# Sequence half of a two-block kernel: two chunks mixed in one operation, and a new order on every engine

## The chip, the cores and the metric

The program runs on one core of a Trainium2 chip. The metric is the device time of the whole program in microseconds (us), as a median of several executions. The matrix engine (TensorE, PE in the rows), the vector engine (VectorE, DVE), the scalar engine (ScalarE, ACT), GpSimd (POOL) and SyncE (SP, which here issues DMAs) each run their own list of instructions in order, and wait for each other by semaphores.

## The reference, cut to what matters

The first half (a spectral gate and a 3x3 convolution) is not touched. Its result z, 512 image rows of 128 positions with 128 channels, goes into the second half:

```python
u = _layernorm(z, ln1_w, ln1_b).reshape(-1, na, e)
y = _mamba2(u, ...)            # below
z = z + _wn_linear(y, ff_g, ff_v, ff_b)
h = gelu(_wn_linear(_layernorm(z, ln2_w, ln2_b), fc1...))
return z + _wn_linear(h, fc2...)

def _mamba2(u):
    z_gate, xBC, dt = split(u @ in_proj_w.T)
    x, Bm, Cm = split(silu(conv1d(xBC, 4 taps) + conv_b))
    dt = softplus(dt + dt_bias);  A = -exp(A_log)
    # scan over positions: h = h*exp(dt*A) + dt*x*B;  y = h.C
    y = _ssm_scan(x, dt, A, Bm, Cm) + D_param * x
    yg = y * silu(z_gate)
    yn = yg * rsqrt(mean(yg**2) + LN_EPS) * ssm_norm_w
    return yn @ out_proj_w.T
```

One row of 128 positions is one sequence ("chunk") with 8 heads of 32 channels and 64 states. The scan is computed as matrices: for each head a 128x128 matrix of decays exp(difference of running sums) times the cross products C.B, and then this matrix times dt*x.

## The kernel before, in words

The sequence half works on groups of four chunks, 128 groups in all. One step of its loop takes one new group in, and holds four groups at different ages: `p` (newest), `a_`, `b`, `c` (oldest). Each engine has a function `body` that lists its operations of one step in a hand-written order; `pipeline` writes out eight steps ahead of the loop, runs the loop with two steps in its body, and writes out the last ones. So the order of `body` is the order on the engine, and every operation begins with waits on semaphores that others raise. `held(...)` is such a wait for a buffer to be free again.

On the path of a group (a number in brackets is the chunk of the four, 0 to 3, or a pair of chunks, 0 or 1):

- DVE `stats_in`, `moments_in`; POOL `root`, `norm_u`: first layer norm. PE `turn_u`, ACT `affine_u`: transposed to `ut`.
- PE `project_x(0)`, `project_x(1)`, `project_bc`, `project_z(0)`, `project_z(1)` (one 128x512 product each) and `project_dt`.
- ACT `tap`, `second_tap`, DVE `taps(j, 2)`, `taps(j, 3)`, POOL `add_tap(j)`: the four taps of the convolution for j = 0, 1 (x) and 2 (B and C); ACT `silu_*`.
- DVE and ACT: the small steps of softplus; PE `cumulate` (running sums), DVE `high`, `low`, `right`, POOL `left`: operands of the decays.
- PE `decays(g)`, ACT `exps(g)`, PE `cross`, DVE `weigh(g)`: the weighted 128x1024 matrix `mmat` of chunk g. PE `turn_x(pair)`, DVE `scale_x(pair)`: `dtx`.
- PE `mix(g)`: eight products of `mmat` and `dtx`, one per head, 32 output partitions each, so four of them stand beside each other in the array. A fp32 product is two instructions in the trace, so a `mix` has 16.
- DVE `gate(pair)`; ACT `squares`, POOL `add_squares`, PE `sums`, DVE `variance`, POOL `root_y`; PE `project_out`; DVE `residual`.
- DVE `stats_mid`, `moments_mid`, POOL `root`, `norm_h`, PE `turn_h`, ACT `affine_h`, PE `ffn1`, ACT `gelu`, PE `ffn2`, DVE `finish`, SP `store`.

The eight PSUM banks are shared by hand: a table of numbers says which product is written to which bank, and several `held` waits exist only because two products share one. In the rows a line number names the operation; on PE L1084 is `mix`, L1013 `project_x`, L1018 `project_bc`, L1027 `project_z`, L1006 `turn_u`, L1109 `turn_h`, L1114 `ffn1`, L1120 `ffn2`, L1053 `turn_x`, L1069 and L1072 `decays`, L1044 `cross`. On DVE L1424 is `residual`, L1315 the statistics, L1329 and L1437 `moments_in` and `moments_mid`, L1345 `add_bias`, L1339 `taps`, L1396 `weigh`, L1406 and L1412 `gate`, L1373 `high`, L1377 `low`, L1382 `right`, L1417 `variance`. On POOL L914 is `add_tap`, L909 `add_squares`, L921 `left`, L955 `add_ffb`, L927 `root_y`, L932 and L934 `root`, L946 and L950 `norm_h`.

## Time and profile before

| | us |
|---|---|
| median of 3 runs | 4249.27 (4245.84 to 4251.49) |
| profiled execution | 4248.45 |
| its span, first to last instruction | 4246.5 |
| granted TensorE clock, mean | 0.976 |

```profile
PE 3975.6 (94%) x31687; PEld 2858.3 (67%) x31687; DVE 3487.8 (82%) x8772; ACT 3152.6 (74%) x4936; POOL 2582.5 (61%) x2713
PE   7998899899989994899999999999999999999998
DVE  4568557754876384899999999999999999999997
ACT  4445534553555253899999999999999999999997
POOL 0036104600560065688888888888888888888886
```

The first row gives busy time, share of the span and instructions of each engine (PEld is the load of a matrix into TensorE, which lies beside PE's products). The others cut the span into 40 equal slices of 106 us; a digit is the busy share in tenths. The sequence half begins in the 17th slice, at about 1700 us, and is even to the end.

### The profile page before, as it was taken

How to read it: one execution, taken by the hardware profiler on the slowest of the kernel's cores; microseconds unless marked ns; L12 is line 12 of the kernel's file. 1: busy time of each engine (PE TensorE's matmuls, PEld its weight loads, DVE VectorE, ACT ScalarE, POOL GpSimd, SP SyncE). 2: the span in 40 equal slices, each digit the busy share in tenths (PEclk: the TensorE clock that was granted, in tenths of full speed). 3: DMA queues.
4: the chain of work that ended last, by engine and by line, in shares of the span. 5: the costliest groups of instructions: out<-in, count | busy, mean ns of one | idle time of the engine just before them, and what ended most of it. 6: DMA issues, size and time to landing. Idle time of an engine off the chain costs nothing.

```text
span 4246.5 us, 94479 instructions
## 1 busy us (share of the span) xinstructions
PE 3975.6 (94%) x31687; PEld 2858.3 (67%) x31687; DVE 3487.8 (82%) x8772; ACT 3152.6 (74%) x4936; POOL 2582.5 (61%) x2713
## 2 busy tenths in 40 slices
PE   7998899899989994899999999999999999999998
PEld 4787578758875883566666666666666666666665
DVE  4568557754876384899999999999999999999997
ACT  4445534553555253899999999999999999999997
POOL 0036104600560065688888888888888888888886
PEclk9999999999999997999999999999999999999999
DMA  2013101400240022111111111111111111111110
GB/s 91 1 53 129 58 9 61 161 11 12 73 157 0 14 85 77 36 40 40 42 40 42 40 37 42 40 42 40 40 39 40 42 40 42 40 37 42 40 42 26
DMA packets 214857, 205.85 MB, mean 48 GB/s; under 512 B 14368, under 2 KB 149152, under 8 KB 214688
## 3 DMA queue, kind: packets, MB, share of 16 engines
q1 hardware_dynamic: 214688, 203.60, 14.8%
q8 instruction: 105, 1.72, 0.2%
q14 instruction: 64, 0.52, 0.0%
HBM read 136.45 MB, written 67.11 MB: 48 GB/s over the span
## 4 chain that ended last, share of the span: by engine, by line
PE 59%; ACT 0%; DVE 0%; POOL 0%; issue 0%; POOLq 0%; DVEq 0%; ACTq 0%
PE g_ps L1084 7%; PE g_ps L1069 6%; PE g_ps L1027 6%; PE g_ps L1013 5%; PE g_ps L1072 5%; PE g_ps L1101 5%; PE g_ps L1044 3%; PE g_ps L1114 3%; PE g_ps L1120 3%; PE g_ps L1093 3%; PE g_ps L1053 3%; PE g_ps L1018 3%; PE g_ps L1033 2%; PE g_ps L1109 2%; PE g_ps L1006 2%; PE g_ps L1038 1%
## 5 line engine op out<-in xcount | busy, mean ns | idle before, releaser
L1396 DVE TENSOR_TENSOR g_mmat<-g_emat,g_ps 128x1024 f32<-128x1024 f32 x512 | 598.9, 1210 | 1.3 <-PE g_ps L1044 1.3
L1235 ACT ACTIVATE g_emat<-g_ps 128x1024 f32<-128x1024 f32 x512 | 521.3, 1025 | 86.3 <-PE g_ps L1072 84.8
L1339 DVE SCALAR_TENSOR_TENSOR g_acc<-g_ps,g_conv_w,g_acc 128x504 f32<-128x504 f32 (+1 forms) x768 | 554.5, 722 | 10.9 <-ACT g_acc L1198 9.2
L914 POOL TENSOR_TENSOR g_acc<-g_acc,g_tap 128x508 f32<-128x508 f32 x384 | 482.2, 1270 | 126.1 <-DVE g_acc L1339 126.1
L654 POOL MEMSET f_s_hi<- 128x192 f32 x4 | 1.0, 258 | 761.0 <-PE f_ps L345 761.0
L1084 PEld LDWEIGHTS g_ps<-g_mmat,g_dtx 128*32 128x32 f32 x8192 | 192.8, 109 | 310.4 <-issue 213.4
L1069 PE MATMUL g_ps<-g_rz,g_l 128*128 128x512 f32 x1024 | 391.3, 463 | 1.6 <-DVE g_z L1424 1.6
L229 PE MATMUL f_ps<-f_s_hi,f_wf_hi 128*128 128x256 f32 x1152 | 360.6, 313 | 4.9 <-DVE f_s_lo L489 4.9
L1084 PE MATMUL g_ps<-g_mmat,g_dtx 128*32 128x128 f32 x8192 | 329.3, 279 | 0.0
L230 PE MATMUL f_ps<-f_s_lo,f_wf_hi 128*128 128x256 f32 x1152 | 326.6, 284 | 0.0
L424 ACT ACTIVATE f_s_hi<-f_ps 128x384 fp32r<-128x384 f32 x256 | 125.6, 491 | 270.5 <-PE f_ps L217 265.2
L231 PE MATMUL f_ps<-f_s_hi,f_wf_lo 128*128 128x256 f32 x1152 | 326.1, 283 | 0.0
L1072 PE MATMUL g_ps<-g_mask_b,g_ident_b 128*128 128x512 bf16 x1024 | 310.7, 385 | 0.0
L672 POOL TENSOR_TENSOR f_zout<-f_zout,f_gamma 128x512 f32<-128x512 f32 x128 | 163.8, 1279 | 240.6 <-ACT f_zout L444 240.1
L1198 ACT ACTIVATE g_acc<-g_ps,g_conv_b,g_conv_w 128x512 f32<-128x512 f32 x384 | 298.4, 777 | 14.5 <-PE g_ps L1018 1.5
L1101 PEld LDWEIGHTS g_ps<-g_wc,g_ygt 128*128 128x128 f32 x2048 | 248.6, 192 | 62.3 <-issue 62.3
L909 POOL TENSOR_TENSOR g_sqs<-g_sq 128x256 f32<-128x256 f32 x256 | 182.0, 731 | 167.8 <-ACT g_sq L1240 167.8
L217 PE MATMUL f_ps<-f_idft_h,f_inv 128*128 128x192 f32 x1024 | 220.6, 341 | 63.7 <-DVE f_s_lo L489 56.6
L934 POOL TENSOR_TENSOR g_r<-g_r,g_mhalf 128x4 f32<-128x4 f32 x256 | 265.4, 1037 | 21.3
L1027 PE MATMUL g_ps<-g_ut,g_wz 128*128 128x512 f32 x512 | 276.2, 621 | 1.7 <-DVE g_acc L1339 1.7
L1013 PE MATMUL g_ps<-g_ut,g_wx 128*128 128x512 f32 x512 | 274.3, 618 | 1.6 <-ACT g_ut L1190 1.6
L1203 ACT ACTIVATE g_tap<-g_ps,g_conv_w 128x512 f32<-128x512 f32 x384 | 262.0, 682 | 2.3 <-PE g_ps L1013 2.2
(193 smaller groups left out, 12319.1 us busy)
## 6 DMA issues: line engine op xcount, KB each, us to landing
f_xt<-in_x_cols SPq DMA_DIRECT2D x32, 1024.0 KB, 10.9
f_xres<-in_x SPq DMA_DIRECT2D x128, 256.0 KB, 2.8
z<-f_zout SPq DMA_DIRECT2D x128, 256.0 KB, 2.0
g_zin<-z SPq DMA_DIRECT2D x128, 256.0 KB, 2.6
g_zres<-z SPq DMA_DIRECT2D x128, 256.0 KB, 2.9
out<-g_outb SPq DMA_DIRECT2D x128, 256.0 KB, 2.9
f_wf_raw<-in_w_f SPq DMA_DIRECT2D x1, 576.0 KB, 7.1
g_wx<-in_in_proj_t SPq DMA_DIRECT2D x1, 192.0 KB, 2.4
```

The source lines that it names most:

```text
L229: pe.matmul(out, wf_hi[:, p, x, :], hi, start=(x == 0), stop=False)
L230: pe.matmul(out, wf_hi[:, p, x, :], lo, start=False, stop=False)
L914: pool.tensor_tensor(acc[:, j, :, 1:], acc[:, j, :, 1:], tap1[:, j, :, 0:P - 1], ALU.add).then_inc(add_p[j], 1)
L1013: pe.matmul(ps[:, X_BANK[j], :], wx[:, j * P:(j + 1) * P], ut[:, :], start=True, stop=True).then_inc(px_mm[j], 1)
L1027: pe.matmul(ps[:, Z_BANK[j], :], wz[:, j * P:(j + 1) * P], ut[:, :], start=True, stop=True).then_inc(pz_mm[j], 1)
L1069: pe.matmul(four(ps[:, D_BANK[g] + half, :]), l4[:, g, :], rz[:, 4 * half:4 * half + 4, :], start=True, stop=False)
L1072: mm = pe.matmul(four(ps[:, D_BANK[g] + half, :]), ident_b[:, :], mask_b[:, :].unsqueeze(1).to_broadcast([P, 4, P]), start=False, stop=True)
L1084: mm = pe.matmul(ps[low:low + HEADDIM, bank, at + j * P:at + (j + 1) * P], dtx[:, g // 2, at + HEADDIM * h:at + HEADDIM * (h + 1)], mmat[: ...
L1101: mm = pe.matmul(ps[:, OUT, g * P:(g + 1) * P], ygt[:, x.s, g, j, :], wc[:, j, :], start=(j == 0), stop=(j == 1))
L1235: act.activation(emat[:, g, :].rearrange("p (b n) -> p b n", b=2), ps[:, D_BANK[g]:D_BANK[g] + 2, :], ACT.Exp).then_inc(e_a[g], 1)
L1339: dve.scalar_tensor_tensor(out=acc[:, j, :, k:], in0=four(ps[:, bank, :])[:, :, 0:P - k], scalar=conv_w[:, j, 3 - k:4 - k], in1=acc[:, j, ...
L1396: dve.tensor_tensor(mmat[:, g, :].rearrange("p (h n) -> p h n", h=HEADS), emat[:, g, :].rearrange("p (h n) -> p h n", h=HEADS), ps[:, CB, ...
```

## The change

`mix` takes a pair of chunks instead of one: it waits for the weighted matrices of both, and issues its 16 products (32 instructions) without a wait in between. There are two of them in a step instead of four, and two semaphores instead of four. All assignments of products to banks but two (`BC_BANK` and `CB`) are changed, with the waits that they need, and every engine's `body` is written in a new order. No arithmetic is added or removed. The diff, cut to its core:

```diff
-        UT, HT, F1 = 5, 5, 0
-        X_BANK, BC_BANK, Z_BANK = (2, 1), 3, (1, 2)
-        CB, XT_BANK, D_BANK, Y_BANK = 6, (4, 2), (0, 0, 4, 4), (3, 4)
-        SS, OUT, F2 = 6, 5, 3
+        UT, HT, F1 = 4, 1, 1
+        X_BANK, BC_BANK, Z_BANK = (1, 0), 3, (5, 2)
+        CB, XT_BANK, D_BANK, Y_BANK = 6, (0, 4), (4, 4, 2, 2), (6, 5)
+        SS, OUT, F2 = 3, 6, 0
...
             def left(x):
                 pool.wait_ge(q_d, x.n + 1)
-                held(pool.wait_ge, sqs_p[1], x.n, QUADS)
-                held(pool.wait_ge, sqs_p[0], x.n, QUADS)
-                pool.wait_ge(add_p[1], x.n + 1)
+                pool.wait_ge(add_p[2], x.n + 1)
...
             def add_ffb(x):
                 pool.wait_ge(zres_in[x.s], x.half * 16 + 16)
+                held(pool.wait_ge, z2_d, x.n, QUADS)
...
             def project_z(x, j):
                 pe.wait_ge(ut_a, x.n + 1)
                 if j == 0:
-                    held(pe.wait_ge, e_a[1], x.n, QUADS)
-                    pe.wait_ge(conv_d[1], x.n * 2 + 2)
-                if j == 1:
-                    pe.wait_ge(conv_d[0], x.n * 2 + 2)
+                    held(pe.wait_ge, gate_d[1], x.n, QUADS)
...
-            def mix(x, g):
-                pe.wait_ge(m_d[g], x.n + 1)
-                pe.wait_ge(dtx_d[g // 2], x.n + 1)
-                if g == 2:
-                    pe.wait_ge(e_a[3], x.n + 1)
+            def mix(x, pair):
+                pe.wait_ge(m_d[2 * pair], x.n + 1)
+                pe.wait_ge(m_d[2 * pair + 1], x.n + 1)
+                pe.wait_ge(dtx_d[pair], x.n + 1)
+                if pair == 1:
+                    pe.wait_ge(e_a[1], x.n + 1)
+                for g in (2 * pair, 2 * pair + 1):
...
-                mm.then_inc(y_mm[g], 1)
+                mm.then_inc(y_mm[pair], 1)
...
             def gate(x, pair):
-                dve.wait_ge(y_mm[2 * pair + 1], x.n + 1)
+                dve.wait_ge(y_mm[pair], x.n + 1)
```

The decays, `turn_x`, `left` and the exponentials now belong to `a_` instead of `b`, that is, they stand at the end of a step instead of the head of the next.

On PE, the stretch of a step that has the mixing, before:

```order
L1013 MATMUL g_ps<-g_ut,g_wx 128x512
L1084 MATMUL g_ps<-g_mmat,g_dtx 32x128 x8
L1109 MATMUL g_ps<-g_ident,g_hn 128x128 x4
L1027 MATMUL g_ps<-g_ut,g_wz 128x512
L1084 MATMUL g_ps<-g_mmat,g_dtx 32x128 x8
L1114 MATMUL g_ps<-g_ht,g_wt 128x512
L1084 MATMUL g_ps<-g_mmat,g_dtx 32x128 x8
L1006 MATMUL g_ps<-g_ident,g_u 128x128 x4
L1084 MATMUL g_ps<-g_mmat,g_dtx 32x128 x8
L1027 MATMUL g_ps<-g_ut,g_wz 128x512
L1120 MATMUL g_ps<-g_wt,g_gl 128x128 x4
```

and now (L1087 is `mix`, L1016 `project_x(1)`, L1021 `project_bc`, L1113 `turn_h`, L1118 `ffn1`, L1123 `ffn2`, L1009 `turn_u`):

```order
L1016 MATMUL g_ps<-g_ut,g_wx 128x512
L1021 MATMUL g_ps<-g_ut,g_wx 128x512
L1027 MATMUL g_ps<-g_ut,g_wz 128x512
L1113 MATMUL g_ps<-g_ident,g_hn 128x128 x4
L1087 MATMUL g_ps<-g_mmat,g_dtx 32x128 x16
L1118 MATMUL g_ps<-g_ht,g_wt 128x512
L1087 MATMUL g_ps<-g_mmat,g_dtx 32x128 x16
L1027 MATMUL g_ps<-g_ut,g_wz 128x512
L1038 MATMUL g_ps<-g_tri,g_dta 128x128
L1123 MATMUL g_ps<-g_wt,g_gl 128x128 x4
L1009 MATMUL g_ps<-g_ident,g_u 128x128 x4
```

Four blocks of mixing have become two, with `ffn1` between them; three 128x512 products now stand side by side, and `turn_u` stands behind `ffn2`.

On DVE, from `low` to `moments_mid`, before:

```order
L1377 SCALAR_TENSOR_TENSOR g_q<-g_hi_10148,g_negm,g_ps 128x128
L1315 BN_STATS g_st_10157<-g_zin 128x6 x4
L1382 TENSOR_TENSOR g_rz<-g_q,g_ps 64x1024
L1339 SCALAR_TENSOR_TENSOR g_acc<-g_ps,g_conv_w,g_acc 128x4x126
L1417 TENSOR_SCALAR g_rsv<-g_ps 128x4
L1329 BN_AGGR g_mv_10159<-g_st_10157 128x2 x4
L1339 SCALAR_TENSOR_TENSOR g_acc<-g_ps,g_conv_w,g_acc 128x4x125
L1388 TENSOR_TENSOR g_dtx<-g_ps,g_dt 128x512
L1424 SCALAR_TENSOR_TENSOR g_z_10126<-g_ps,g_ry,g_zresb 128x128 x4
L1315 BN_STATS g_st_10158<-g_z_10126 128x6 x4
L1345 TENSOR_TENSOR g_ps<-g_ps,g_dtb 128x32
L1437 BN_AGGR g_mv_10160<-g_st_10158 128x2 x4
```

and now (L1369 is `low`, L1374 `right`, L1436 `finish`, L1409 `variance`, L1307 the statistics, L1416 `residual`, L1337 `add_bias`, L1321 `moments_in`, L1429 `moments_mid`):

```order
L1369 SCALAR_TENSOR_TENSOR g_q<-g_hi_10148,g_negm,g_ps 128x128
L1374 TENSOR_TENSOR g_rz<-g_q,g_ps 64x1024
L750 ISA
L1436 TENSOR_TENSOR g_outb<-g_ps,g_z2b 128x512
L1409 TENSOR_SCALAR g_rsv<-g_ps 128x4
L1307 BN_STATS g_st_10157<-g_zin 128x6 x4
L1380 TENSOR_TENSOR g_dtx<-g_ps,g_dt 128x512
L1416 SCALAR_TENSOR_TENSOR g_z_10126<-g_ps,g_ry,g_zresb 128x128 x4
L1337 TENSOR_TENSOR g_ps<-g_ps,g_dtb 128x32
L1317 REGISTER_ALU
L1321 BN_AGGR g_mv_10159<-g_st_10157 128x2 x4
L1307 BN_STATS g_st_10158<-g_z_10126 128x6 x4
```

`right` follows `low`, whose result it reads, at once; two operations stand between `residual` and the statistics that read it; and the step (and the loop) ends at `variance`.

On POOL, one step from `norm_u` on, now (L940 is its last part, L914 `add_tap`, L909 `add_squares`, L919 `left`, L925 `root_y`, L954 `add_ffb`, L930 and L932 `root` of the second layer norm):

```order
L914 TENSOR_TENSOR g_acc<-g_acc,g_tap_10134 128x4x127
L909 TENSOR_TENSOR g_sqs<-g_sq 128x256
L914 TENSOR_TENSOR g_acc<-g_acc,g_tap_10134 128x4x127
L909 TENSOR_TENSOR g_sqs<-g_sq 128x256
L914 TENSOR_TENSOR g_acc<-g_acc,g_tap_10134 128x4x127
L919 TENSOR_TENSOR g_l_10151<-g_q,g_ind_g 64x512
L925 TENSOR_TENSOR g_ry<-g_rsv,g_mhalf 128x4
```

Before, the three `add_tap` stood together ahead of both `add_squares`, and `left`, `add_ffb` and `root_y` followed. Now the two kinds alternate, and `left` and `root_y` stand directly behind `add_tap(2)`.

## Rows read from the trace of the kernel before

**Rows 1.** Windows: busy us (instructions) of each engine in 2000 us, then PE clock.
```profile
2000.00:4000.00 2000.00, 2000.00 (x16123) 1306.02 (x16123) 1942.26 (x5003) 1882.39 (x2756) 1662.61 (x1736) 1.00 0.13 40
```

**Rows 2.** Timeline, PE: start, length, line, operation, count; one step's ends and its mixing.
```profile
3004.37 1.02 PE L1013 MATMUL g_ps<-g_ut,g_wx 128*128 128x512 f32 x2
3005.33 0.64 PE L1084 MATMUL g_ps<-g_mmat,g_dtx 128*32 128x128 f32 x16
3005.90 0.66 PE L1109 MATMUL g_ps<-g_ident,g_hn 128*128 128x128 f32 x4
...
3016.84 1.02 PE L1018 MATMUL g_ps<-g_ut,g_wx 128*128 128x512 f32 x2
3017.70 0.60 PE L1053 MATMUL g_ps<-g_ident,g_xs 128*128 128x128 f32 x4
...
3023.97 1.02 PE L1013 MATMUL g_ps<-g_ut,g_wx 128*128 128x512 f32 x2
```

**Rows 3.** Timeline, PE: where two mixings met, near the end of the span.
```profile
4204.31 1.08 PE L1084 MATMUL g_ps<-g_mmat,g_dtx 128*32 128x128 f32 x32
4205.32 1.13 PE L1027 MATMUL g_ps<-g_ut,g_wz 128*128 128x512 f32 x2
```

**Rows 4.** Timeline, DVE: starts and lengths, with and without gaps between operations.
```profile
2998.82 1.13 DVE L1424 SCALAR_TENSOR_TENSOR g_z<-g_ps,g_ry,g_zresb 128x128 f32<-128x128 f32 x4
3000.08 0.87 DVE L1315 BATCH_NORM_STATS2 g_st<-g_z 128x6 f32<-128x128 f32 x4
3000.87 0.18 DVE L1345 TENSOR_TENSOR g_ps<-g_ps,g_dtb 128x32 f32<-128x32 f32 x1
3001.11 0.38 DVE L1437 BATCH_NORM_AGGREGATE g_mv<-g_st 128x2 f32<-128x6 f32 x4
...
3008.74 0.73 DVE L1339 SCALAR_TENSOR_TENSOR g_acc<-g_ps,g_conv_w,g_acc 128x500 f32<-128x500 f32 x1
...
3012.30 0.69 DVE L1412 TENSOR_TENSOR g_ygt<-g_ps,g_zs 128x512 f32<-128x512 f32 x1
3012.99 0.29 DVE L1373 CAST g_hi<-g_ps 128x128 fp32r<-128x128 f32 x1
3013.20 0.68 DVE L1444 TENSOR_TENSOR g_outb<-g_ps,g_z2b 128x512 f32<-128x512 f32 x1
3013.79 0.33 DVE L1377 SCALAR_TENSOR_TENSOR g_q<-g_hi,g_negm,g_ps 128x128 fp32r<-128x128 f32 x1
3014.05 0.86 DVE L1315 BATCH_NORM_STATS2 g_st<-g_zin 128x6 f32<-128x128 f32 x4
3014.83 1.20 DVE L1382 TENSOR_TENSOR g_rz<-g_q,g_ps 64x1024 fp32r<-64x1024 f32 x1
...
3016.61 0.16 DVE L1417 TENSOR_SCALAR g_rsv<-g_ps 128x4 f32<-128x4 f32 x1
3016.85 0.38 DVE L1329 BATCH_NORM_AGGREGATE g_mv<-g_st 128x2 f32<-128x6 f32 x4
...
3017.77 0.68 DVE L1388 TENSOR_TENSOR g_dtx<-g_ps,g_dt 128x512 f32<-128x512 f32 x1
```

**Rows 5.** Timeline, POOL, with idle time before an operation and who ended it.
```profile
3001.68 0.23 POOL L932 TENSOR_SCALAR g_r<-g_mv 128x4 f32<-128x4 f32 x1 [0.37 <-DVE g_mv L1437]
...
3009.55 2.50 POOL L914 TENSOR_TENSOR g_acc<-g_acc,g_tap 128x508 f32<-128x508 f32 x2 [0.91 <-DVE g_acc L1339]
3013.31 1.42 POOL L909 TENSOR_TENSOR g_sqs<-g_sq 128x256 f32<-128x256 f32 x2 [1.26 <-ACT g_sq L1240]
3014.81 1.04 POOL L921 TENSOR_TENSOR g_l<-g_q,g_ind_g 64x512 fp32r<-64x512 f32 x1
3016.03 1.27 POOL L955 TENSOR_TENSOR g_zresb<-g_zres,g_ffb 128x512 f32<-128x512 f32 x1 [0.19 <-POOL g_l L921]
```

**Rows 6.** Timeline near the end: POOL `root_y` and the DVE `residual` that waits for it.
```profile
4228.87 1.02 POOL L927 TENSOR_TENSOR g_ry<-g_rsv,g_mhalf 128x4 f32<-128x4 f32 x1 [0.65 <-DVE g_rsv L1417]
4229.98 1.13 DVE L1424 SCALAR_TENSOR_TENSOR g_z<-g_ps,g_ry,g_zresb 128x128 f32<-128x128 f32 x4 [1.19 <-POOL g_ry L927]
```

More of the change, by code:

```diff
@@ L965, in body @@
                 if b:
-                    left(b)
+                    add_ffb(b)
                 if c:
-                    add_ffb(c)
-                    root_y(c)
+                    root(c, r2, mv2, mv2_d, r2a_p, r2_p)
+                    norm_h(c)
                 if p:
@@ L978, in body @@
                 if a_:
-                    add_tap(a_, 2)
                     add_tap(a_, 0)
+                if b:
+                    add_squares(b, 1)
+                if a_:
                     add_tap(a_, 1)
@@ L983, in body @@
                     add_squares(b, 0)
-                    add_squares(b, 1)
+                if a_:
+                    add_tap(a_, 2)
+                    left(a_)
+                if b:
+                    root_y(b)
             pipeline(pool, QUADS, body)
@@ L1151, in body @@
                 if b:
-                    mix(b, 2)
+                    mix(b, 0)
+                if a_:
+                    project_z(a_, 0)
+                    cumulate(a_)
+                if c:
+                    ffn2(c)
                 if p:
@@ L1155, in body @@
                 if b:
-                    mix(b, 3)
+                    project_out(b)
+                    sums(b)
+                if p:
+                    project_x(p, 0)
                 if a_:
-                    project_z(a_, 1)
-                if c:
-                    ffn2(c)
+                    turn_x(a_, 1)
+                if p:
+                    project_dt(p)
                 if a_:
-                    cumulate(a_)
+                    turn_x(a_, 0)
+                    decays(a_, 2)
+                    decays(a_, 0)
+                    cross(a_)
+                    decays(a_, 3)
+                    decays(a_, 1)
                 if p:
                     project_x(p, 1)
-                if b:
-                    project_out(b)
-                    sums(b)
+                    project_bc(p)
             pipeline(pe, QUADS, body)
@@ L1452, in body @@
                 if b:
-                    right(b)
+                    scale_x(b, 1)
+                if c:
+                    residual(c)
                 if a_:
-                    taps(a_, 1, 2)
-                if c:
-                    variance(c)
+                    add_bias(a_)
                 if p:
                     moments_in(p)
-                if a_:
-                    taps(a_, 1, 3)
+                if c:
+                    stats_mid(c)
                 if b:
@@ L1464, in body @@
                 if c:
[L1465 to L1469 removed]
                     moments_mid(c)
                 if a_:
[L1472 to L1476 removed]
+                    taps(a_, 0, 2)
                 if b:
                     weigh(b, 0)
+                if a_:
+                    taps(a_, 0, 3)
+                if b:
                     weigh(b, 2)
@@ L1482, in body @@
                 if b:
-                    weigh(b, 1)
                     weigh(b, 3)
                 if a_:
-                    taps(a_, 0, 2)
+                    positive(a_)
                     rounding(a_)
-                    positive(a_)
-                    taps(a_, 0, 3)
+                if b:
+                    weigh(b, 1)
+                if a_:
+                    taps(a_, 1, 2)
                     step_size(a_)
+                if b:
+                    gate(b, 1)
+                if a_:
+                    taps(a_, 1, 3)
+                    exponent(a_)
                 if b:
@@ L1493, in body @@
                 if a_:
-                    exponent(a_)
-                if b:
-                    gate(b, 1)
-                if a_:
+                    taps(a_, 2, 2)
                     high(a_)
+                    taps(a_, 2, 3)
+                    low(a_)
+                    right(a_)
                 if c:
                     finish(c)
+                if b:
+                    variance(b)
             pipeline(dve, QUADS, body)
```

139 lines of the change are left out of this document (52 added, 87 removed).

## The prediction

> **What bounds the kernel now.** I read the slices of the page first: the change leaves the first half alone, so only the stretch from 1700 us on counts. Then the windows [rows 1]: in 2000 us of it TensorE is busy 2000.00 us at the full clock (1.00, that is 2.4 GHz), DVE 1942.26, ACT 1882.39, POOL 1662.61. TensorE never stops, so the length of a step is the sum of its products. The same product begins at 3004.37 and at 3023.97 [rows 2]: a step is 19.60 us. The loop and the written-out steps that run at that pace are about 126 of the 128.
>
> DVE is nearly full too. Its 97% is not slack of 3%: the missing share is gaps between two operations, and they must be sorted by cause before a new order can be priced. Normally an operation starts 0.07 to 0.08 before the end of the one ahead (L1377 is 0.33 long and the next starts 0.26 later; L1444, 0.68 and 0.59). The exceptions [rows 4]: `residual` to the statistics that read it, 1.26 for a length of 1.13, so 0.13 after the end instead of 0.08 before, 0.21 lost; `add_bias` to `moments_mid`, 0.24 for a length of 0.18, 0.14 lost to the same kind of wait (`moments_mid` reads the statistics just ahead); `gate` to `high`, 0.69 for a length of 0.69, 0.08 lost, since `high` waits for TensorE's `cumulate`; `variance` to `moments_in`, 0.24 for 0.16, 0.16 lost. Together 0.59, and a few hundredths elsewhere, so DVE's own work is 19.60 - 0.61 = 18.99 us a step.
>
> **The change part by part.**
>
> *Joined mixing.* A block of 16 instructions takes 0.57 from its start to the next one's (3005.33 to 3005.90 [rows 2]), so two take 1.14. Near the end two blocks met, and the 32 took 1.01 (4204.31 to 4205.32 [rows 3]). A pair saves 0.13, two pairs 0.26. There are also fewer borders between mixing and full-width products: a 128x512 product takes 0.96 next to a mixing (3004.37 to 3005.33) and 0.86 between others (3016.84 to 3017.70). `project_x` and `project_z(1)` lose that neighbour, 2 x 0.10. TensorE's own work falls to 19.60 - 0.26 - 0.20 = 19.14 us a step, and a little less, as `turn_u` also loses two such borders, which I do not count. Nothing else on PE is added: the same products, in another order, with its two loads of 0.1 exposed where it enters and leaves a mixing.
>
> The row of a mixing is where a rule can be weighed. The second 16 instructions of a joined block take 0.44 where the first 16 alone take 0.57, so their loads find something to overlap with [rows 2, 3]. The Trainium skill ("TensorE: Matmul & The Clock Gate", Part 3, on what overlaps) says that a weight load overlaps a running matmul only if it is for another row group. All heads use all rows here, so by that rule nothing is pulled ahead, a joined block costs two separate ones, 1.14, and TensorE would fall by 0.20 alone, to 19.40. The trace decides for 1.01.
>
> *DVE.* The new order takes away the 0.21 behind `residual` (`add_bias` and `moments_in` stand between), the 0.14 before `moments_mid` (`scale_x(0)` stands between) and the wait of `high`. It adds two things. `right` now stands directly behind `low` and reads it: by the 0.13 after the end that the dependent pair shows, 0.21. And the step ends at `variance`, only 0.16 long, with the loop's branch behind it every second step; before, the 0.68 of `finish` covered that. The trace has no row for it: it is at least 0 and at most 0.5 per two steps by the nearest row, the 0.16 behind the same `variance` when its wait ended late, tripled for the branch's instructions. I take 0.3 per two steps, 0.15 a step. DVE: 18.99 + 0.21 + 0.15 = 19.35. `add_bias` (0.18 long) is now followed by `moments_in` with two waits and a register operation. Its price lies between 0 and 0.14 (the gap behind it now, [rows 4]); I take 0, since a full microsecond of `residual` stands ahead in which DVE's waits can be worked off, and keep 0.14 for the range.
>
> On the chip's side a page disagrees on that 0.21. The Trainium skill ("VectorE: DVE Perf Modes", section "The DRAIN you can't avoid") says that chained operations pay the same with a semaphore between them or without. By it `right` behind `low` costs nothing and DVE needs 19.14. The rows show 0.21 between a dependent pair and an independent one [rows 4]. What follows does not hang on it, as the next loop is longer than either.
>
> *Loops through several engines.* A step can't be shorter than any closed chain from one operation back to itself a step later. Three matter, all through `residual`.
>
> (a) `residual` to `taps(2, 3)` on DVE, then POOL `add_tap(2)`, `left`, `root_y`, and `residual` of the next group, which waits for `root_y`. On DVE that is its own work less what stands outside: `taps(2, 3)` 0.65, `low` 0.26, `right` 1.12, `finish` 0.59, `variance` 0.08, the statistics 0.78, `scale_x` 0.60 (each its length less 0.08, or the start of the next [rows 4]), together 4.08: 18.99 - 4.08 = 14.91. `taps` to POOL: 3008.74 to 3009.55, 0.81 [rows 4, 5]. `add_tap` is half of 2.50, 1.25, and `left` waits for it: between 1.25 and 1.44 (with the 0.19 of the dependent POOL pair [rows 5]); I take 1.40. `left` to the next, 3014.81 to 3016.03, 1.22. `root_y` to `residual`, 1.11 [rows 6]. Sum 14.91 + 0.81 + 1.40 + 1.22 + 1.11 = 19.45.
>
> (b) `residual` to `moments_mid` on DVE, then nearly all of POOL. POOL's own work is 19.60 less its waits of 0.37, 0.91, 1.26 and 0.19 [rows 5] and some 0.07 at L921, 16.8; less `add_ffb` 1.24 (it fits into the wait behind `residual`), plus 0.15 for `left` behind `add_tap(2)` and 0.11 for `root_y` to `residual`: 15.82. DVE: `residual` 1.05, `add_bias` 0.10, `moments_in` 0.30, statistics 0.79, `scale_x` 0.60, and 3001.11 to 3001.68 for `moments_mid` to POOL, 0.57: 3.41. Sum 19.23.
>
> (c) `gate(1)` to PE's `project_z(0)`, which now waits for it (bank 5 is shared), and through `turn_x`, the decays, `exps(0)` and `weigh(0)` back to `gate(1)`. Estimated from the starts of the same step: `gate(1)` to PE 1.85, PE to the end of the second decays 9.8, `exps` 1.05, DVE 6.2: 18.9. It is not the longest, but PE will stand at `project_z(0)` for what is left over, some 0.3 to 0.5 a step. Behind it are `cumulate`, `ffn2`, `turn_u`, `project_out`, `sums`; their readers on DVE come 0.2 or more later than they need.
>
> So (a) sets the pace: 19.45 against 19.35 (DVE alone), 19.23 and 19.14 (PE). ACT's 1882 of 2000 leaves it over a microsecond; the three table loads stay three. DMA is moved nowhere on SP; the load of `zres` waits for `add_ffb`, which comes two thirds of a step earlier than its reader needs.
>
> **The sum.** 19.60 - 19.45 = 0.15 a step, x 126 = 18.9 us. The filling and the drain hold the same chains in the same order, 0. The profiled execution took 4248.45, so 4248.45 - 18.9 = 4229.6; the median of the runs is 0.8 above it. I forecast 4230.
>
> **Rivals.**
>
> - *The exposed waits cost nothing*: `left` starts at 1.25 and the branch is hidden. Then (a) is 19.30 and DVE 19.20, a gain of 0.30 x 126 = 38: 4211. For it: POOL runs independent operations at 1.25. Against: both dependent pairs in the rows wait. 0.22.
> - *No difference that shows*: `add_bias` costs its 0.14 and (a) becomes 19.59. TensorE's gain is then all a wait at `project_z(0)`: 4247. For it: the gap behind the same operation in [rows 4], though another cause explains it there. 0.15.
> - *POOL becomes the bound, slower*: its four changes between `add_tap` and `add_squares` have no row, since equal operations stood together before (2.50 for two, 1.42 for two). If each costs 0.19, as the dependent pair, (b) is 19.23 + 0.76 = 19.99, and 0.39 x 126 = 49: 4297; at 0.13 each it is 19.75 and 4267. It decides from 0.10 each. Against: POOL's waits on others' semaphores that are long raised cost nothing in the rows. Taken at 4267, 0.10.
> - *TensorE still sets the pace*: the whole saving of PE comes through, 0.46 x 126 = 58: 4190. It needs (a) and DVE both 0.3 shorter than summed, which no row supports. 0.03.
>
> **How the numbers follow.** My case has 0.50, by itself 4222 to 4240. A measurement of this kernel tells 0.2%, 8.5 us, from no change, so faster means under 4241. Faster: nine tenths of 0.50, 0.22 and 0.03 and a little of the third case, 0.73. Same: the rest of mine and most of the third, 0.16. Slower 0.11. The range leaves out the last case and most of the slow one: 4208 to 4249.
>
> **What would show it right or wrong.** In the changed profile a step is 19.4 to 19.5; mixing has 32 instructions in 1.0 us; PE's busy time falls below its window for the first time, with one wait a step at L1027 for DVE's `gate`; DVE's `residual` waits for POOL `root_y`, POOL has no wait between `root` and `left` but a small one for `taps(2, 3)`; `right` starts 0.13 after `low` ends. If PE waits nowhere and a step is still over 19.5, the cost of its borders is wrong; if DVE waits for `sums`, `turn_x` or the exponentials, a chain through PE is longer than (c); if POOL is gapless, it is the rival. A step of 19.2 would mean that the dependent starts are cheap.

## The result, and the profile after

The changed kernel took 4202.31 us (median of 4 runs, 4200.05 to 4204.69), the kernel before 4248.35 (4 runs beside them, 4245.84 to 4251.49). The ratio is 0.9891, 95% interval 0.9874 to 0.9908: faster by 1.1%, 46 us. I had forecast 4230 with a range of 4208 to 4249, so the direction was right and the time lies below the range. The profiled execution took 4203.05 (span 4200.9) against 4248.45 (span 4246.5).

The window over 2000 us of the steady steps, as in [rows 1] (columns: the stretch, then busy us and count of PE, PEld, DVE, ACT and POOL, granted clock, DMA share, GB/s):

```profile
2000.00:4000.00 2000.00, 1966.38 (x16395) 1351.78 (x16395) 1955.37 (x5093) 1911.77 (x2806) 1695.54 (x1766) 1.00 0.13 41
```

TensorE was busy 2000.00 before and is now busy 1966.38: it is no longer the engine that never stops. Its clock is the same full one. All others got busier, since more steps fit. DVE issues 49 instructions a step, so 5093 / 49 = 103.9 steps in 2000 us; averaged over the starts of one operation in about 102 of these steps, a step is 19.254 us against 19.595 (all step lengths below are such averages). 0.341 x 126 = 43.0 us of the 45.4 between the two profiled executions; the other 2.4 are in the filling and the drain.

TensorE around the mixing, to be held against [rows 2, 3] (L1087 is `mix`, L1118 `ffn1`, L1027 `project_z`, L1016 `project_x`, L1054 `turn_x`):

```profile
2998.50 1.02 PE L1027 MATMUL g_ps<-g_ut,g_wz 128*128 128x512 f32 x2
2999.36 0.60 PE L1113 MATMUL g_ps<-g_ident,g_hn 128*128 128x128 f32 x4
2999.89 1.08 PE L1087 MATMUL g_ps<-g_mmat,g_dtx 128*32 128x128 f32 x32
3000.90 1.13 PE L1118 MATMUL g_ps<-g_ht,g_wt 128*128 128x512 f32 x2
3001.96 1.08 PE L1087 MATMUL g_ps<-g_mmat,g_dtx 128*32 128x128 f32 x32
3003.36 1.10 PE L1027 MATMUL g_ps<-g_ut,g_wz 128*128 128x512 f32 x2 [0.32 <-DVE g_ygt L1404]
```

A joined mixing takes 1.01 from its start to the next product's (2999.89 to 3000.90), as the one near the end did before. `project_z(1)` stands between full-width products and takes 0.86 (2998.50 to 2999.36). `project_z(0)` waits 0.32 for DVE's `gate(1)`.

The waits of the same 2000 us (engine, line waited at, releaser: us in total, times, longest; weight loads and others left out):

```profile
POOL g_zresb L954 <- DVE g_z L1416: 138.0, 104, 1.4
POOL g_r L930 <- DVE g_mv L1429: 85.5, 104, 0.9
...
PE g_ps L1027 <- DVE g_ygt L1404: 33.6, 104, 0.3
DVE g_z L1416 <- issue: 6.1, 37, 0.2
DVE g_z L1416 <- POOL g_ry L925: 2.5, 15, 0.2
```

The last two rows are small and easily passed over. They are the only waits of DVE, and DVE's `residual` (L1416) is where they stand. The page counts idle time only from the end of the operation ahead; from start to start, `scale_x` to `residual` is 0.75 on the average where the same `scale_x` before another operation is 0.59.

DVE and POOL through that wait, to be held against [rows 4 to 6]. DVE (L1369 `low`, L1374 `right`, L1436 `finish`, L1409 `variance`, L1307 the statistics, L1380 `scale_x`, L1416 `residual`, L1337 `add_bias`, L1321 `moments_in`, L1429 `moments_mid`; the L1331 row is `taps(2, 3)`):

```profile
3006.43 0.73 DVE L1331 SCALAR_TENSOR_TENSOR g_acc<-g_ps,g_conv_w,g_acc 128x500 f32<-128x500 f32 x1
3007.08 0.34 DVE L1369 SCALAR_TENSOR_TENSOR g_q<-g_hi,g_negm,g_ps 128x128 fp32r<-128x128 f32 x1
3007.45 1.21 DVE L1374 TENSOR_TENSOR g_rz<-g_q,g_ps 64x1024 fp32r<-64x1024 f32 x1
3008.59 0.67 DVE L1436 TENSOR_TENSOR g_outb<-g_ps,g_z2b 128x512 f32<-128x512 f32 x1
3009.19 0.14 DVE L1409 TENSOR_SCALAR g_rsv<-g_ps 128x4 f32<-128x4 f32 x1
3009.26 0.85 DVE L1307 BATCH_NORM_STATS2 g_st<-g_zin 128x6 f32<-128x128 f32 x4
3010.04 0.67 DVE L1380 TENSOR_TENSOR g_dtx<-g_ps,g_dt 128x512 f32<-128x512 f32 x1
3010.87 1.13 DVE L1416 SCALAR_TENSOR_TENSOR g_z<-g_ps,g_ry,g_zresb 128x128 f32<-128x128 f32 x4 [0.16 <-issue]
3011.91 0.19 DVE L1337 TENSOR_TENSOR g_ps<-g_ps,g_dtb 128x32 f32<-128x32 f32 x1
3012.01 0.37 DVE L1321 BATCH_NORM_AGGREGATE g_mv<-g_st 128x2 f32<-128x6 f32 x4
3012.30 0.84 DVE L1307 BATCH_NORM_STATS2 g_st<-g_z 128x6 f32<-128x128 f32 x4
```

POOL in the same stretch (L914 `add_tap`, L909 `add_squares`, L919 `left`, L925 `root_y`, L954 `add_ffb`):

```profile
3004.43 0.73 POOL L909 TENSOR_TENSOR g_sqs<-g_sq 128x256 f32<-128x256 f32 x1
3005.12 1.28 POOL L914 TENSOR_TENSOR g_acc<-g_acc,g_tap 128x508 f32<-128x508 f32 x1
3006.41 0.73 POOL L909 TENSOR_TENSOR g_sqs<-g_sq 128x256 f32<-128x256 f32 x1
3007.24 1.26 POOL L914 TENSOR_TENSOR g_acc<-g_acc,g_tap 128x508 f32<-128x508 f32 x1
3008.65 1.04 POOL L919 TENSOR_TENSOR g_l<-g_q,g_ind_g 64x512 fp32r<-64x512 f32 x1
3009.77 1.02 POOL L925 TENSOR_TENSOR g_ry<-g_rsv,g_mhalf 128x4 f32<-128x4 f32 x1
3012.14 1.28 POOL L954 TENSOR_TENSOR g_zresb<-g_zres,g_ffb 128x512 f32<-128x512 f32 x1 [1.36 <-DVE g_z L1416]
```

Loop (a) can be read off link by link. `taps(2, 3)` 3006.43 to `add_tap(2)` 3007.24: 0.81. To `left` 3008.65: 1.41. To `root_y` 3009.77: 1.12. To `residual` 3010.87: 1.10. From this `residual` to the `taps(2, 3)` of the next step, 3006.43 + 19.25 = 25.68: 14.81. The five add up to 19.25, the step. Every closed path does that, so the sum alone proves nothing. What speaks for this path is that each link is as short as it is where its reader is known to wait: `add_tap` starts 0.81 behind the `taps` that it waits for, here and in [rows 4, 5]; `left` starts 0.14 behind the end of `add_tap(2)`, which it waits for; `root_y` 0.08 behind the end of `left`, its neighbour ahead; `residual` 1.11 on the average behind the start of `root_y` in both kernels; and from `residual` to `taps(2, 3)` no wait of DVE's for another engine is to be seen. The experiments test it.

### The profile page after: what moved, and what is told of

The parts are those of the page before. It is cut to its first block and busy times, and to the rows that moved or that the text cites. A ratio compares the mean times of both kernels' runs of the same rounds, so it can differ in the third digit from the quotient of the medians.

```text
span 4200.9 us, 93784 instructions
## 1 busy us (share of the span) xinstructions
PE 3889.3 (93%) x31687; PEld 2885.8 (69%) x31687; DVE 3461.5 (82%) x8772; ACT 3147.3 (75%) x4936; POOL 2587.3 (62%) x2713
## 5 line engine op out<-in xcount | busy, mean ns | idle before, releaser
L1388 DVE TENSOR_TENSOR g_mmat<-g_emat,g_ps 128x1024 f32<-128x1024 f32 x512 | 618.0, 1208 | 2.5 <-ACT g_emat L1228 2.5
L1228 ACT ACTIVATE g_emat<-g_ps 128x1024 f32<-128x1024 f32 x512 | 496.2, 1021 | 88.6 <-PE g_ps L1073 87.1
L1331 DVE SCALAR_TENSOR_TENSOR g_acc<-g_ps,g_conv_w,g_acc 128x504 f32<-128x504 f32 (+1 forms) x768 | 558.2, 727 | 1.8 <-ACT g_tap L1196 1.8
L914 POOL TENSOR_TENSOR g_acc<-g_acc,g_tap 128x508 f32<-128x508 f32 x384 | 488.5, 1272 | 17.4 <-DVE g_acc L1331 4.7
L1027 PE MATMUL g_ps<-g_ut,g_wz 128*128 128x512 f32 x512 | 272.0, 613 | 42.0 <-DVE g_ygt L1404 42.0
L1087 PEld LDWEIGHTS g_ps<-g_mmat,g_dtx 128*32 128x32 f32 x8192 | 208.5, 110 | 120.1 <-issue 120.1
L932 POOL TENSOR_TENSOR g_r<-g_r,g_mhalf 128x4 f32<-128x4 f32 x256 | 265.4, 1037 | 21.3
L1087 PE MATMUL g_ps<-g_mmat,g_dtx 128*32 128x128 f32 x8192 | 277.3, 276 | 0.8 <-issue 0.8
L954 POOL TENSOR_TENSOR g_zresb<-g_zres,g_ffb 128x512 f32<-128x512 f32 x128 | 163.4, 1277 | 168.8 <-DVE g_z L1416 168.7
L1016 PE MATMUL g_ps<-g_ut,g_wx 128*128 128x512 f32 x512 | 264.1, 598 | 1.7 <-ACT g_ut L1185 1.7
L1105 PE MATMUL g_ps<-g_wc,g_ygt 128*128 128x128 f32 x2048 | 250.0, 276 | 1.5 <-DVE g_ygt L1404 1.5
```

Source lines behind the costliest of these rows:

```text
L914: pool.tensor_tensor(acc[:, j, :, 1:], acc[:, j, :, 1:], tap1[:, j, :, 0:P - 1], ALU.add).then_inc(add_p[j], 1)
L1027: pe.matmul(ps[:, Z_BANK[j], :], wz[:, j * P:(j + 1) * P], ut[:, :], start=True, stop=True).then_inc(pz_mm[j], 1)
L1087: mm = pe.matmul(ps[low:low + HEADDIM, Y_BANK[pair], at + j * P:at + (j + 1) * P], dtx[:, pair, at + HEADDIM * h:at + HEADDIM * (h + 1)], ...
L1228: act.activation(emat[:, g, :].rearrange("p (b n) -> p b n", b=2), ps[:, D_BANK[g]:D_BANK[g] + 2, :], ACT.Exp).then_inc(e_a[g], 1)
L1331: dve.scalar_tensor_tensor(out=acc[:, j, :, k:], in0=four(ps[:, bank, :])[:, :, 0:P - k], scalar=conv_w[:, j, 3 - k:4 - k], in1=acc[:, j, ...
L1388: dve.tensor_tensor(mmat[:, g, :].rearrange("p (h n) -> p h n", h=HEADS), emat[:, g, :].rearrange("p (h n) -> p h n", h=HEADS), ps[:, CB, ...
```

## The experiments

Thirteen kernels, each run beside the kernel before on the same chip. Ratios are to the kernel before, with their 95% intervals. The kernel before took 4248.35 to 4250.57 beside them, and an interval is 4 to 10 us to either side. So where two kernels differ by less, the step lengths, each an average over about 100 steps of one profiled execution, tell more than the times.

| kernel | step, us | median, us | ratio |
|---|---|---|---|
| before | 19.595 | 4248.35 | 1 |
| changed | 19.254 | 4202.31 | 0.9891 (0.9874 to 0.9908) |
| b_join | 19.63 | 4255.71 | 1.0017 (1.0008 to 1.0027) |
| b_join2 | 19.33 | 4216.09 | 0.9920 (0.9898 to 0.9943) |
| b_dve | 20.39 | 4345.26 | 1.0228 (1.0211 to 1.0245) |
| b_both | 20.48 | 4357.53 | 1.0254 (1.0237 to 1.0271) |
| a_two | 19.257 | 4205.40 | 0.9898 (0.9882 to 0.9915) |
| a_three | 19.33 | 4210.36 | 0.9907 (0.9891 to 0.9924) |
| a_gap | 19.50 | 4233.57 | 0.9969 (0.9956 to 0.9981) |
| a_in | 19.36 | 4216.36 | 0.9926 (0.9906 to 0.9946) |
| a_out | 19.26 | 4204.27 | 0.9895 (0.9876 to 0.9914) |
| a_rooty | 19.67 | 4254.20 | 1.0012 (1.0002 to 1.0022) |
| a_rooty2 | 19.31 | 4211.01 | 0.9908 (0.9891 to 0.9924) |
| a_moments | 19.240 | 4201.39 | 0.9889 (0.9873 to 0.9906) |
| a_halves | 19.182 | 4194.74 | 0.9865 (0.9849 to 0.9882) |

Kernels with b_ start from the kernel before, those with a_ from the changed one.

### Parts of the change on the kernel before

**b_join**: the mixings stand in pairs, nothing else is changed.

```diff
-    mix(b, 0)             # ahead of turn_h
     turn_h(c)
     project_z(a_, 0)
+    mix(b, 0)
     mix(b, 1)
     ffn1(c)
     mix(b, 2)
+    mix(b, 3)
     turn_u(p)
-    mix(b, 3)
```

> The kernel before, with nothing but TensorE's order changed: the four mixings of a step stand as two adjacent pairs. If TensorE's sum alone set the 19.60 us step, the step falls to 19.14 and the time to about 4190. If DVE's own row with its gaps stands right behind it (19.60 less the 0.1 that it waited for cumulate), the step stops at 19.45 to 19.50, the time is 4232 to 4236, and TensorE waits about 0.3 us a step.

Neither came: 4255.71. TensorE's own work did fall by what was summed, to a busy share of 1952.34 in 2000 us (19.63 x 0.976 = 19.16 a step), but the row of `turn_h` shows where it went:

```profile
3010.01 0.63 PE L1109 MATMUL g_ps<-g_ident,g_hn 128*128 128x128 f32 x4 [0.47 <-ACT g_emat L1233]
```

Without `mix(0)` ahead of it, `turn_h` comes 0.5 us earlier to a PSUM bank that ACT has not yet read. An operation that I took away as time was also the cover of a wait.

**b_join2**: the same, with `project_z(0)` ahead of `turn_h`.

```diff
-    mix(b, 0)
-    turn_h(c)
     project_z(a_, 0)
+    turn_h(c)
+    mix(b, 0)
     mix(b, 1)
     ffn1(c)
     mix(b, 2)
+    mix(b, 3)
     turn_u(p)
-    mix(b, 3)
```

> The kernel before with the mixings joined in pairs, and project_z(0) ahead of turn_h, so that TensorE has work while ACT finishes exps(3), for which turn_h waits (that wait took the gain in b_join). TensorE's sum is again 19.14 us a step. Theory: DVE's row with its gaps is the second bound in the old order, so the step is 19.46 to 19.52 and the time 4231 to 4239. Rival: joined mixing pays in full once nothing waits, step 19.15, 4192. Second rival: another wait of the old order turns up and it is 4248 again.

4216.09, between the two. The window, columns as before:

```profile
2000.00:4000.00 2000.00, 1991.03 (x16354) 1320.05 (x16356) 1951.96 (x5068) 1910.61 (x2794) 1691.42 (x1759) 1.00 0.13 41
```

TensorE now waits 9 us in 2000. DVE is all but gapless, with the gaps behind `residual` and before `moments_mid` of [rows 4] still in its row, and only 0.05 a step of waiting, ahead of `residual` (from `scale_x` to it 0.65 on the average, where 0.60 is the least). I had expected 19.46 because I counted the gaps at `high` and `variance` as DVE's own. They were not: `variance` started 0.04 behind the end of TensorE's `sums` before and starts 0.29 behind it now, and both gaps are gone with TensorE's order as the only change. So the joined mixings, with one product placed as cover, give 0.27 of the 0.34 us a step without any of DVE's new order.

**b_dve** and **b_both**: DVE's order around `residual` alone, and together with b_join's.

```diff
     variance(c)
-    moments_in(p)
...
     residual(c)
-    stats_mid(c)
     add_bias(a_)
+    moments_in(p)
+    stats_mid(c)
+    scale_x(b, 1)
     moments_mid(c)
...
-    scale_x(b, 1)
```

> The kernel before, with nothing but DVE's order around residual changed: add_bias and moments_in stand between residual and stats_mid, scale_x(1) between stats_mid and moments_mid. DVE's gaps fall by about 0.35 us a step. As TensorE sets the pace, no change: 19.60 a step, 4248. If DVE's gaps also counted, up to 0.35 x 126 = 44 us less.

> Both edits together on the kernel before, with its old bank assignments, its old loops and POOL order. If the gain is the sum of TensorE's 0.46 and DVE's 0.35 being taken away side by side, the step is about 19.15 to 19.25 and the time 4192 to 4205, that is all of the measured gain. If the new order of POOL and ACT or the new banks are needed for it, it stays near 19.45 and 4232.

Both missed widely: 4345.26 and 4357.53. The waits of b_dve:

```profile
POOL g_r L932 <- DVE g_mv L1329: 175.8, 98, 1.8
...
PE g_ps L1109 <- POOL g_hn L950: 70.8, 98, 0.8
```

`moments_in` moved behind `residual` is late for POOL's `root(p)`, and in the order of before the rest of POOL's step is queued behind that `root`. The changed kernel asks POOL for `root(c)` and `norm_h` first. That DVE's order is good only together with this one is an argument from the two rows; no run gives the kernel before both, or the changed kernel the old table of banks.

### What joins a mixing

**a_three**: the changed kernel with four mixings again, two of them apart, as before the change: `mix(2)`, `project_z(1)`, `mix(3)`, `ffn1`, `mix(0)`, `mix(1)`.

> The changed kernel with the mixing cut again: four operations with their own waits, chunks 2 and 3 with project_z(1) between them, 0 and 1 adjacent. TensorE's own work rises by about 0.13 for the split and 0.1 to 0.2 for the borders. If the loop residual, taps(2,3), add_tap(2), left, root_y sets the 19.25 us step, TensorE's wait at project_z(0) shrinks from about 0.4 and the time stays within 5 us of 4202. If TensorE's shorter sum is what the time follows, it rises by 0.25 to 0.35 x 126, to 4235 to 4245.

4210.36: 8 us slower than the changed kernel (the theory said at most 5), far from the rival's 4235. TensorE is busy 2000.00 of 2000 again and a step is 19.33, against the 0.983 x 19.254 = 18.93 that it is busy in the changed kernel. So 0.40 us a step of TensorE's were given back, and only 0.08 of them show. With no idle time left, TensorE sets the pace here again. Held against b_join2, this tells what the two halves of the change are worth: joined mixings alone reach 19.33, the new orders and banks without them 19.33 too (that the two are equal is chance), and both together 19.254.

**a_two**: all four mixings in their places, but each an operation with waits of its own, side by side in pairs.

```diff
-    mix(b, 1)             # 32 instructions, waits ahead of the first alone
+    mix(b, 2)
+    mix(b, 3)
...                        # the same for the other pair
```

> The changed kernel with each joined mixing written again as two operations of 16 matmuls, one right behind the other, with their own waits. Theory (the matmuls overlap wherever they stand side by side, and a step is set by the chain through residual and root_y): TensorE's row costs at most 0.1 a step more, and the time stays within 4 us of 4202. Rival (the joining itself is worth the 0.13 us for each of two): 0.26 a step on TensorE, 19.1 to 19.2, still hidden: 4202 to 4208.

4205.40 and 19.257, TensorE busy 1966.00: as the changed kernel. What saves time is that the mixings are neighbours. Writing them as one operation saves nothing that shows (0.003 us a step).

### Which chain holds the changed kernel

**a_gap**: `stats_mid` directly behind `residual`.

```diff
     residual(c)
+    stats_mid(c)
     add_bias(a_)
     moments_in(p)
-    stats_mid(c)
```

> The changed kernel with stats_mid directly behind residual, as it was before; add_bias and moments_in follow it. Theory (loop residual, taps(2,3), add_tap(2), left, root_y sets the pace, and all of it on DVE lies in the loop): the dependent start costs 0.2 a step more, 19.45, 4227. Rival (TensorE or POOL's long stretch behind moments_mid sets the pace): under 0.05 a step, within 6 us of 4202.

4233.57, and 0.246 us a step: the whole of the gap shows, as it must for DVE work that lies between `residual` and `taps(2, 3)`.

**a_in** and **a_out**: the same copy of 128x32 (0.10 us from start to start, into a buffer that nobody reads) at two places of DVE's row. a_in has it behind `step_size`, between `residual` and `taps(2, 3)`; a_out has it behind `taps(2, 3)`, where only DVE's own row has to carry it.

```diff
     step_size(a_)
+    filler(a_)            # a_in
...
     taps(a_, 2, 3)
+    filler(a_)            # a_out
     low(a_)
```

> The changed kernel with one more DVE copy of 128x32 (0.10 us, its result unused) behind step_size, which lies between residual and taps(2,3), inside the loop. Theory: 0.10 a step, 12.6 us: 4215. Rival (another chain is the longest): less than 0.05 a step, under 6 us.

> The same copy, behind taps(2,3) and ahead of low, so that it lies on DVE but outside the loop; DVE waits 0.16 us a step for root_y at residual, and that wait takes the 0.10. Theory of the loop: no change, 4202 within 3. Rival (DVE's row alone is the bound, its waits being gaps that can't be used): 0.10 a step as in the other place, 4215.

4216.36 and 4204.27; a step 0.106 longer and 0.006 longer. DVE does the same work in both, so its own row isn't the bound. Loop (b) leaves DVE at `moments_mid` and doesn't hold the place of a_in. Loop (c) does, but it has room of 0.14 or more: at its link from the exponentials to `weigh(0)`, DVE starts 0.24 behind their end, in the changed kernel as in a_in, and only 0.10 behind it in a_rooty (below), where it has to wait. Loop (a) is left. This pair is the plainest evidence of the study.

**a_rooty**: POOL's `root_y` ahead of `left`, so that `left` is no longer in the loop.

```diff
     add_tap(a_, 2)
-    left(a_)
     root_y(b)
+    left(a_)              # with one more wait, for root_y's end
```

> The changed kernel, with POOL's root_y of a chunk ahead of its left of the next, which cuts the closed chain residual, taps(2,3), add_tap(2), left, root_y open: root_y no longer stands behind left. Theory: another chain then closes at once, since root_y now stands behind DVE's variance and left behind it: variance to root_y 0.24, root_y and left to DVE's decays 2.1, decays(2) and (0) 2.1, exps(0) 1.05, and from there to the next variance 13.9: about 19.4 a step, 4215 to 4225. Rival (the changed kernel's pace is DVE's own row and nothing else): left is a little late, but the time stays within 5 us of 4202.

4254.20, the theory's sign and more than its size. The chain that it named can be followed in POOL's, ACT's and DVE's rows, of which the ones at its links are:

```profile
3000.14 1.94 ACT L1230 ACTIVATE g_emat<-g_ps 128x1024 f32<-128x1024 f32 x2 [0.29 <-PE g_ps L1075]
...
3016.07 0.14 DVE L1411 TENSOR_SCALAR g_rsv<-g_ps 128x4 f32<-128x4 f32 x1
3016.30 1.02 POOL L926 TENSOR_TENSOR g_ry<-g_rsv,g_mhalf 128x4 f32<-128x4 f32 x1 [0.77 <-DVE g_rsv L1411]
...
3017.49 1.04 POOL L920 TENSOR_TENSOR g_l<-g_q,g_ind_g 64x512 fp32r<-64x512 f32 x1 [0.17 <-POOL g_ry L926]
...
3019.81 1.94 ACT L1230 ACTIVATE g_emat<-g_ps 128x1024 f32<-128x1024 f32 x2 [0.29 <-PE g_ps L1075]
```

`variance` to `root_y` 0.23, to `left` 1.19, to the exponentials 2.32 (through TensorE's decays), and 15.93 from the exponentials to the next `variance`: 19.67, the step. DVE now waits too, 0.49 a step on the average ahead of `weigh(0)`, for the exponentials and for TensorE's `cross`, which end 0.02 apart. The 1.19 holds 0.17 for the wait that the edit adds to `left`, so a part of what this kernel loses is not the order's.

**a_rooty2**: the same, and `variance` ahead of `finish`.

```diff
     right(a_)
+    variance(b)
     finish(c)
-    variance(b)
...                        # and a_rooty's edit
```

> The same, and DVE's variance of the chunk ahead of finish, so that root_y can start about half a microsecond earlier. Theory: the first chain is cut and the second has about 18.8 a step, so that DVE's own row, 19.09 a step in the changed kernel with its wait for root_y taken off, becomes the pace: 19.10 to 19.15 a step, 4183 to 4190, faster than both kernels. Rival (the new chain through variance, root_y and left still sets the pace): 4202 or above.

4211.01, a miss. `residual` waits for nothing any more, but `variance` does. It stands directly behind `right`, and reads the sums that TensorE (L1099) has only just made:

```profile
3012.31 1.10 PE L1029 MATMUL g_ps<-g_ut,g_wz 128*128 128x512 f32 x2 [0.18 <-DVE g_ygt L1406]
...
3016.40 1.21 DVE L1376 TENSOR_TENSOR g_rz<-g_q,g_ps 64x1024 fp32r<-64x1024 f32 x1
...
3016.58 1.06 PE L1099 MATMUL g_ps<-g_ones,g_sqs 128*128 128x128 f32 x8
...
3017.68 0.16 DVE L1411 TENSOR_SCALAR g_rsv<-g_ps 128x4 f32<-128x4 f32 x1
```

The sums end at 3017.64 and `variance` starts at 3017.68, 1.28 behind `right`, which alone takes 1.14. TensorE has no pause from L1029 to there, and L1029 waits for DVE's `gate(1)`: a loop of DVE and TensorE. `finish`, 0.60 us long, had been its cover.

**a_moments**: `moments_in` ahead of `residual`, into its wait.

```diff
     scale_x(b, 1)
+    moments_in(p)
     residual(c)
     add_bias(a_)
-    moments_in(p)
     stats_mid(c)
```

> The changed kernel with DVE's moments_in (four instructions, 0.29 us from start to start) ahead of residual, in whose 0.16 us of waiting for root_y a part of it fits, instead of behind it. Theory (the chain residual, taps(2,3), add_tap(2), left, root_y sets the pace): the chain loses 0.29 us and gains at most 0.10, since stats_mid then has only add_bias between itself and residual: at most 19.07 a step. DVE's own row, 19.09 plus 0 to 0.10, becomes the pace: 19.1 to 19.2 a step, 4183 to 4195, faster than the changed kernel. Rival (the wait for root_y only goes to where another transfer is late, as when root_y was put first): 4199 or above.

4201.39: no difference from the changed kernel that shows in the times (a step is 0.01 shorter), so the forecast of a faster one was wrong. The wait for `root_y` is gone, as expected (`moments_in` to `residual` is 0.29 on the average, its length less 0.08), but not at the price that I gave the other side. DVE around `residual`:

```profile
3011.89 1.10 DVE L1416 SCALAR_TENSOR_TENSOR g_z<-g_ps,g_ry,g_zresb 128x128 f32<-128x128 f32 x4
3012.90 0.19 DVE L1337 TENSOR_TENSOR g_ps<-g_ps,g_dtb 128x32 f32<-128x32 f32 x1
3013.14 0.88 DVE L1307 BATCH_NORM_STATS2 g_st<-g_z 128x6 f32<-128x128 f32 x4
```

`add_bias` to the statistics is 0.24 here and 0.10 before `moments_in` in the changed kernel. `residual` to the statistics is 1.25, and 1.27 in a_gap with nothing between them, where an independent operation follows `residual` after 1.04. So the statistics start 0.21 to 0.24 us later than an independent operation would, and 0.10 of `add_bias` in that room covers 0.10 of it.

**a_halves**: two instructions of `moments_in` ahead of `residual`, two behind `add_bias`.

```diff
     scale_x(b, 1)
+    moments_in(p)         # chunks 0 and 1
     residual(c)
     add_bias(a_)
-    moments_in(p)
+    moments_in_2(p)       # chunks 2 and 3
     stats_mid(c)
```

> The changed kernel with moments_in in two halves: two instructions (0.155 us) ahead of residual, in its wait for root_y, two behind add_bias. With all four ahead, the wait was gone (0.237 instead of 0.267 us for residual's first part) but stats_mid then stood 0.14 us idle behind add_bias, the step was 19.240 instead of 19.254, and the time the same. Theory (the chain through residual and root_y and DVE's row with what lies between residual and stats_mid are two bounds of nearly one height): with half ahead the chain is 19.10, the space behind residual 0.10 + 0.13 = 0.23 us against 0.235 that it takes, so no idle time is left in either place: 19.10 to 19.12 a step, 4183 to 4187. Rival (a third bound stands close under the present pace): 4196 to 4203.

4194.74, ratio 0.9865 (0.9849 to 0.9882), below the changed kernel's 0.9891: its four runs (4189.59 to 4196.29) all lie below the changed kernel's (4200.05 to 4204.69). The intervals of the two ratios overlap by a little; the steps, 19.182 and 19.254, differ by 0.072, and x 126 that is 9 us. It is the fastest kernel here, 7.6 us below the changed one, about half of what I expected. DVE's row:

```profile
3008.04 0.24 DVE L1321 BATCH_NORM_AGGREGATE g_mv<-g_st 128x2 f32<-128x6 f32 x2
3008.30 1.13 DVE L1420 SCALAR_TENSOR_TENSOR g_z<-g_ps,g_ry,g_zresb 128x128 f32<-128x128 f32 x4
3009.34 0.19 DVE L1341 TENSOR_TENSOR g_ps<-g_ps,g_dtb 128x32 f32<-128x32 f32 x1
3009.44 0.24 DVE L1325 BATCH_NORM_AGGREGATE g_mv<-g_st 128x2 f32<-128x6 f32 x2
3009.59 0.86 DVE L1307 BATCH_NORM_STATS2 g_st<-g_z 128x6 f32<-128x128 f32 x4
```

No idle time is left between `residual` and the statistics. The step is 19.182 instead of 19.10, because in every second step `residual` still waits 0.10 for `root_y`. The loop's branch stands behind `variance` in the other steps and makes DVE later by 0.17; in the steps without it, POOL is the later one. From `taps(2, 3)` to `residual` DVE needs 4.36 or 4.52, POOL's chain 4.45: the mean of the later ones is 4.49, not 4.45. With DVE's 14.68 that is 19.17. The next bound may be close, but no run tests it: `weigh(0)` starts 0.11 behind the end of the exponentials here, 0.24 in the changed kernel, and 0.10 in a_rooty, where it waits.

## Why the prediction was wrong

**The step that failed** is the sum of loop (a): "14.91 + 0.81 + 1.40 + 1.22 + 1.11 = 19.45". The mechanism stands: that loop, link by link, is the step, and a_in, a_out and a_gap show it by experiment. Its sum was 0.20 too long, and 0.20 x 126 = 25 us is nearly all of the 28 between 4230 and 4202 (most of the rest is the 2.4 of the filling and the drain, which I put at 0). Two terms carry it:

- `left` to `root_y` was given 1.22 and measured 1.12. I took it from `left` to `add_ffb` in [rows 5], whose start has a wait of its own in brackets, 0.19. The length of `left` plus the 0.08 to 0.1 that POOL needs between neighbours would have been right.
- DVE from `residual` to `taps(2, 3)` was given 14.91 and measured 14.81. It was made from 18.99, a whole row less what stands outside, and 18.99 from gaps sorted by hand, with every row rounded to 0.01. Averaged over 101 steps of the kernel before, the gaps come to 0.66 where I had sorted out 0.61 (`residual` 0.23, `add_bias` 0.14, `high` 0.10, `variance` 0.18, and 0.02 ahead of `residual`), and with these averages the term is 14.87: 0.04 of the error. The other 0.06 are operations that were shorter afterwards, as the first instruction behind a late wait is: the statistics of `stats_mid` 0.757 for 0.790, `moments_in` and `moments_mid` 0.286 for 0.296 each, `scale_x` 0.590 for 0.598.

The other terms: `taps` to POOL 0.81 (0.81), `add_tap` to `left` 1.41 (1.40), `root_y` to `residual` 1.10 (1.11).

**TensorE.** The joined mixing costs 1.01, as taken from [rows 3], and the full-width products 0.86. Its work a step is at most 18.93 where 19.14 was summed; the borders of `turn_u`, which I named and left out, are a part of that: from its start to the next product's it took 0.585 and takes 0.437, averaged over the steps. It waits once a step, 0.32 at L1027 (0.3 to 0.5 forecast), and does not bound anything. The rival "TensorE still sets the pace" (4190) is refuted by those 33.6 us of waits. The rule of the Trainium skill ("TensorE: Matmul & The Clock Gate", Part 3), that a weight load overlaps a running matmul only when the row group differs, does not hold here. But I had the wrong row against it. The weight loads (PEld) of one mixing before and of a joined one now are:

```profile
3005.32 0.38 PEld L1084 LDWEIGHTS g_ps<-g_mmat,g_dtx 128*32 128x32 f32 x16 [0.76 <-issue]
2999.89 0.81 PEld L1087 LDWEIGHTS g_ps<-g_mmat,g_dtx 128*32 128x32 f32 x32 [0.17 <-issue]
```

The products of the same mixings start at 3005.33 [rows 2] and 2999.89, so the loads of a block of 16 lay beside its running products already, all on the same 128 rows. In both blocks four matrices are loaded while the four products ahead run, and each four start 0.11 behind the last. Sixteen instructions are four such fours, 0.44; the 0.13 more that a block costs are spent once, at its ends. Joining saves one block's ends, and not, as the prediction read it, loads that found nothing to overlap with before. a_two and a_three add that only the neighbourhood counts.

**DVE.** 19.35 was forecast for its own work; 19.09 is measured (19.254 less the 0.16 that `residual` waits). Three errors of 0.10, 0.07 and 0.10 make the difference. 18.99 was 0.10 too much, as above. The branch was given 0.15 a step and costs 0.08: `variance` to the statistics is 0.07 and 0.24 in turns, 0.15 on the average, but the 0.07 are there without a branch. `add_bias` cost nothing, as taken. `right` behind `low` was priced at 0.21 by the wrong pair: it starts 0.03 after `low` ends (3007.08 + 0.34, 3007.45), so it loses 0.11 where 0.21 was taken. The Trainium skill's sentence ("VectorE: DVE Perf Modes", "The DRAIN you can't avoid") that a semaphore between chained operations costs nothing extra does not carry over to a wait for the operation directly ahead: read as in the prediction it gives `right` for nothing, and it costs those 0.11.

**POOL.** The slower rival (4267) is dead: `add_tap` and `add_squares` in turn run at 1.29 (3005.12 to 3006.41) and 0.83 between their starts, and the 0.83 holds the wait for `taps(2, 3)`, which starts 0.81 before. Loop (b) isn't binding, as said, and that wait shows it: from `add_squares(0)` to `add_tap(1)`, the same two kinds, it is 0.69 (3004.43 to 3005.12), so the end of POOL's long stretch has 0.14 a step to spare. The waits of 1.36 and 0.8 behind `residual` and `moments_mid` show nothing of the kind, since they are where loop (b) itself passes from DVE to POOL.

**The rival that came nearest**, "the exposed waits cost nothing" at 4211, is not what happened: `left` did start 1.41 behind `add_tap`, and the branch was paid, if only with 0.08. It was near by its number alone, which was luck.

**The range.** Its lower end, 4208, was the price of one rival mechanism, rounded. It had no room for an error in the sum of loop (a) itself, made of some twenty rounded rows and one interval with a foreign wait in it. An error of 0.1 us in a step is 12.6 us here; the sum was off by two of these, and the rival's own sum, from the same rows, could be off as far below 4211.
